# Two turns of a software pipeline written into each pass of the loop, on one Trainium2 core

## The reference

```python
x = layer_norm(inputs); q, k, v = x @ wq, x @ wk, x @ wv          # 16 heads of 16
out_i = phi(q_i) . cumsum(phi(k_j) v_j^T) / (phi(q_i) . cumsum phi(k_j))   # causal, phi = relu + 0.001
x = out @ wo + inputs; x = x + gelu(layer_norm(x) @ w1) @ w2
x = layer_norm(x + ffn(quantise_to_fp6_grid(x)))                   # blocks of 32
q, k, v = silu(conv4(x @ Wq)), silu(conv4(x @ Wk)), silu(conv4(x @ Wv))
delta = chunkwise delta rule over chunks of 32 (inverse of I + A per chunk), 4 heads of 64
short, long = causal FIR filters of 5 and 64 taps on v
y = gated mix of (short, long, delta, v) by an MLP on statistics; y = layer_norm(rms(y) @ Wo + x)
first 1024 tokens: y = layer_norm(y + mixture-of-experts MLP with 2048 hidden)
```

## Time and profile before

| | |
|---|---|
| median of 3 runs | 6195.41 us (6194.68 to 6212.29) |
| profiled execution: its own time | 6197.09 us |
| its span in the profile | 6195.3 us |
| busy: PE, weight loads, DVE, ACT, POOL | 5461.0, 4375.8, 4265.9, 2703.4, 2545.4 us |
| mean granted TensorE clock | 0.915 |

### The profile page before, as it was taken

The page is one execution under the profiler, slowest core; times in us unless marked ns, Lnnn a source line. Parts: engine busy times, 40 slices in busy tenths (PEclk is TensorE's granted clock), DMA queues, the critical chain, the costliest instruction groups (busy, mean ns, idle before and its releaser), DMA issues. The chain is left out here.

```text
span 6195.3 us, 137128 instructions
## 1 busy us (share of the span) xinstructions
PE 5461.0 (88%) x42776; PEld 4375.8 (71%) x42776; DVE 4265.9 (69%) x13841; ACT 2703.4 (44%) x6230; POOL 2545.4 (41%) x3716
## 2 busy tenths in 40 slices
PE   6999999999999999969875528999999999999947
PEld 5888888888888888859844426776767667676734
DVE  4777777777777777732157775887878778787830
ACT  2555555555555555521143313444444444444421
POOL 1222222222222222200087734666666666666640
PEclk9999999999999999979955557999999999999978
DMA  1101110111011101138755522222222222222201
GB/s 40 34 30 34 35 35 28 34 35 35 30 32 35 35 31 32 33 79 193 183 139 134 141 80 66 59 60 60 60 60 60 61 60 60 60 60 60 60 16 41
DMA packets 604094, 374.75 MB, mean 60 GB/s; under 512 B 336528, under 2 KB 589264, under 8 KB 603344
## 3 DMA queue, kind: packets, MB, share of 16 engines
q1 hardware_dynamic: 532880, 329.91, 19.6%
q10 hardware_dynamic: 65664, 16.78, 1.2%
q0 software_dynamic: 4800, 18.88, 1.0%
HBM read 212.59 MB, written 137.10 MB: 56 GB/s over the span
## 5 line engine op out<-in xcount | busy, mean ns | idle before, releaser
L510 POOL TENSOR_TENSOR a_shift<-a_mean_var,a_eps 128x2 f32<-128x2 f32 x256 | 71.3, 279 | 1933.9 <-DVE a_mean_var L725 1933.9
L2141 PE MATMUL c_bank<-c_xT,c_gate 128*128 128x512 f32 x1024 | 508.9, 621 | 17.9 <-issue 16.6
L739 DVE SCALAR_TENSOR_TENSOR a_cv<-a_raw,a_taps,a_cv 128x256 f32<-128x256 f32 x1152 | 461.8, 478 | 20.9 <-DVE a_scaled L668 11.1
L811 PE MATMUL a_bank<-a_w,a_hidden 128*128 128x256 f32 x2048 | 459.2, 383 | 0.9 <-ACT a_hidden L599 0.9
L909 PE MATMUL a_bank<-a_turned,a_w 128*128 128x256 f32 x2048 | 454.4, 380 | 1.3 <-ACT a_turned L558 1.1
L811 PEld LDWEIGHTS a_bank<-a_w,a_hidden 128*128 128x128 f32 x2048 | 384.4, 190 | 71.3 <-issue 20.5
L909 PEld LDWEIGHTS a_bank<-a_turned,a_w 128*128 128x128 f32 x2048 | 384.6, 190 | 54.2 <-ACT a_turned L558 5.1
L1783 POOL TENSOR_TENSOR c_expd<-c_e,c_logit 128x16 f32<-128x16 f32 x128 | 371.7, 2904 | 64.0 <-DVE c_logit L1969 52.8
L1769 POOL TENSOR_TENSOR c_stats<-c_l2sq,half 128x16 f32<-128x16 f32 x128 | 373.5, 2918 | 17.4 <-DVE c_l2sq L1958 17.4
L2145 PEld LDWEIGHTS c_bank<-c_statsT,c_gate_stats 128*128 128x128 f32 x2048 | 271.9, 193 | 126.9 <-issue 126.9
L1343 POOL TENSOR_TENSOR i_coef<-i_base,i_exponent 128x12 f32<-128x12 f32 x128 | 297.8, 2327 | 91.7 <-ACT i_base L1373 87.4
(11 more groups left out here) (295 smaller groups left out, 14072.2 us busy)
## 6 DMA issues: line engine op xcount, KB each, us to landing
a_x<-in_x SPq DMA_DIRECT2D x64, 256.0 KB, 4.0
scratch_xb<-a_xb SPq DMA_DIRECT2D x64, 256.0 KB, 2.1
scratch_q<-a_qkv_rows SPq DMA_DIRECT2D x64, 256.0 KB, 2.2
scratch_k<-a_qkv_rows SPq DMA_DIRECT2D x64, 256.0 KB, 2.5
scratch_v<-a_qkv_rows SPq DMA_DIRECT2D x64, 256.0 KB, 2.8
b_window<-scratch_v SPq DMA_DIRECT2D x8, 2048.0 KB, 22.3
scratch_long<-b_out ACTq DMA_DIRECT2D x8, 2048.0 KB, 24.6
scratch_short<-b_out POOLq DMA_DIRECT2D x8, 2048.0 KB, 18.4
```

The costliest lines, as they stand in the source:

```text
L739: ins = dve.scalar_tensor_tensor(cv[s][:, n, c], raw[s][:, n, c, j:j + TOK], taps[:, n, c, j:j + 1], cv[s][:, n, c], ALU.mult, ALU.add)
L811: ins = pe.matmul(dst[:, t * D:(t + 1) * D], src[s][:, c, tile_cols(t)], weight[:, c], start=(c == 0), stop=(c == chunks - 1))
L2141: pe.matmul(dst[:].rearrange("p (h t) -> p h t", h=H), gate1[:, c, cols], xT[sl][:, c:c + 1].broadcast_to([P, H, P]), start=(c == 0), stop ...
```

## The change

`run_pipelined` writes `written=2` turns into the body of each loop. The loop counts passes from 0, and `(iterations - last) // 2` of them are run: 7 in phase A, 3 in phase I, 3 in phase C. A turn that is left over (one in phase A, one in phase C) is written out behind the loop with constants. `skip` is gone, and `PsumPlan.left_out` takes the jobs that a first or last turn lacks out of the counts.

```diff
+def run_pipelined(eng, order, iterations, stages, link=None, links=None, written=1):
...
-            elif skip is not None:
-                skip(j - late, s, stage)
...
-    with eng.Fori(last, iterations) as j:
+    passes = (iterations - last) // written
+    if passes > 1:
+        with eng.Fori(0, passes) as n:
+            for m in range(written):
+                turn(n * written + (last + m), range(last + 1), base + (n * written + m) * each)
+    for j in range(last + passes * written if passes > 1 else last, iterations):
         turn(j, range(last + 1), base + (j - last) * each)
...
+    def left_out(self, b, turn, rank):
+
+        first = self.turns if not isinstance(turn, int) else turn
+        n = sum(late > t for t in range(min(first, self.turns)) for late in self.lates[b])
+        if not isinstance(turn, int):
+            return n
+        n += sum(late < t - self.iterations + 1 for t in range(self.iterations, turn) for late in self.lates[b])
+        return n + sum(late > turn or late < turn - self.iterations + 1 for late in self.lates[b][:rank])
+
     def free(self, i, s, job):
-        b = self.bank_of[s, job]
-        return (i + self.late[s, job]) * self.uses[b] + (self.base[b] + self.rank[s, job])
+        b, turn, rank = self.bank_of[s, job], i + self.late[s, job], self.rank[s, job]
+        return turn * self.uses[b] + (self.base[b] + rank - self.left_out(b, turn, rank))
...
-        return [base + (iterations + self.turns) * uses for base, uses in zip(self.base, self.uses)]
+        return [base + iterations * uses for base, uses in zip(self.base, self.uses)]
...
-            def skip(i, s, stage):
-
-                for job in jobs_of.get(stage, ()):
-                    b = plan.bank(s, job)
-                    open_bank(i, s, job)
-                    pe.sem_inc(bank_full[b], 1)
-                    pe.sem_inc(bank_read[b], 1)
-
-            run_pipelined(pe, order, batches, stages, skip=skip)
+            run(pe, order, batches, stages)
```

More of the change, by code:

```diff
@@ L11 @@
 from contextlib import ExitStack
+from functools import partial
 import math
@@ L98, in __init__ @@
         self.bank_of, self.rank, self.late, self.uses = {}, {}, {}, [0] * BANKS
+        self.lates = [[] for _ in range(BANKS)]
         for n, (stage, s, late, job) in enumerate(jobs):
@@ L251, in phase_a @@
     T = 2
+    WRITTEN = 2
     DEPTH = 4.779
@@ L271, in phase_a @@
               ("lnB_stats", 1.69), ("lnB", 1.72), ("xbT", 3.97), ("qkv1", 3.91), ("conv", 1.64), ("qkvT", 0.01)]
+    run = partial(run_pipelined, written=WRITTEN)
     order = pipelined(shares, STEPS, DEPTH)
@@ L497, in store_qkv @@
                     sp.dma_start(out_v[name][i * STEPS + s], qkv_rows[s][:, n]).then_inc(qkv_stored[s % OUTS], 16)
-            run_pipelined(sp, order, batches, {"load": load, "lnB": store_xb, "qkvT": store_qkv})
+            run(sp, order, batches, {"load": load, "lnB": store_xb, "qkvT": store_qkv})
             for m in range(OUTS):
@@ L537, in _ @@
             link = Chain(pool, S["pool_chain"])
-            run_pipelined(pool, order, batches, stages, link, links)
+            run(pool, order, batches, stages, link, links)
         @block.scalar
@@ L636, in _ @@
             }
-            run_pipelined(act, order, batches, stages)
+            run(act, order, batches, stages)
         @block.vector
@@ L764, in _ @@
             link = Chain(dve, S["dve_chain"])
-            run_pipelined(dve, order, batches, stages, link, links)
+            run(dve, order, batches, stages, link, links)
         @block.tensor
@@ L1186, in phase_i @@
               ("kT", 0.01), ("gram", 2.87), ("keep", 269.02), ("gather", 11.45), ("inverse", 6.78)]
+    run = partial(run_pipelined, written=WRITTEN)
     order = pipelined(shares, STEPS, DEPTH)
     jobs_of = {"xT": ["xT"], "beta": ["beta"], "kT": ["kT"], "gram": ["G0", "G1"]}
-    plan = PsumPlan(order, jobs_of, banks.count)
+    plan = PsumPlan(order, jobs_of, banks.count, ITERATIONS)
     steps_of = [[0]] + [[2 * s - 1, 2 * s] for s in range(1, STEPS)]
@@ L1327, in store_inverse @@
                       .then_inc(S["inverse_stored"], 16)
-            run_pipelined(sp, order, ITERATIONS, {"load": load, "scale": store_coef, "keep": store_below,
+            run(sp, order, ITERATIONS, {"load": load, "scale": store_coef, "keep": store_below,
                                                   "gather": gather, "inverse": store_inverse})
@@ L1429, in _ @@
             link = Chain(dve, S["dve_chain"])
-            run_pipelined(dve, order, ITERATIONS, {"squares": sums, "keep": keep, "inverse": invert}, link, links)
+            run(dve, order, ITERATIONS, {"squares": sums, "keep": keep, "inverse": invert}, link, links)
         @block.tensor
@@ L1479, in gram @@
                                 fill(ins, s, f"G{o}")
[L1481 to L1489, removed]
+            run(pe, order, ITERATIONS, {"xT": turn_x, "beta": beta, "kT": turn_k, "gram": gram})
     banks.count = plan.after(ITERATIONS)
@@ L1747, in store @@
                     sp.dma_start(xc_v[i], xc[sl][:]).then_inc(xc_stored, 16)
-            run_pipelined(sp, order, TILES, {"load": load, "load_src": load_sources, "lnD": store})
+            run(sp, order, TILES, {"load": load, "load_src": load_sources, "lnD": store})
             for m in range(OUTS):
@@ L1810, in _ @@
             link = Chain(pool, N["pool_chain"])
-            run_pipelined(pool, order, TILES, stages, link, {"rms": 1, "lnC_stats": 3, "lnD_stats": 3})
+            run(pool, order, TILES, stages, link, {"rms": 1, "lnC_stats": 3, "lnD_stats": 3})
         @block.scalar
@@ L1893, in _ @@
                 stages[f"solve{b}"] = solved(b)
-            run_pipelined(act, order, TILES, stages)
+            run(act, order, TILES, stages)
         @block.vector
@@ L2179, in _ @@
                 stages[f"carry{b}"] = carry(b)
[L2181 to L2189, removed]
+            run(pe, order, TILES, stages)
     banks.count = plan.after(TILES)
```

18 lines of the change are left out of this document (10 added, 8 removed).

## The result

The changed kernel takes 6090.74 us (median of 4 runs, 6087.91 to 6109.03) against 6195.05 us (median of 4, 6194.49 to 6212.29): ratio 0.9831, 95% interval 0.9806 to 0.9857. 104 us are gained, 1.7%, where 62 were forecast, and the fast end of the range was 6115 us: the prediction was wrong. Run again later (run 9), the same code gave 0.9852 (0.9834 to 0.9869). The profiled execution took 6089.46 us; its span is 107.6 us shorter than that of the kernel before.

The account below looks back on a forecast made before the run. TensorE was taken to bound phases A and C, with VectorE the engine to watch in phase I. 40.5 + 15.8 + 2 + 0 + 2.3 + 1.5 = 62.1 us off 6195.4 gave 6133 us, range 6115 to 6166 us.

Parts of the forecast that it names:

- In phase C's last turns gaps of up to 0.75 us end at `skip`: End of phase C: dropping `skip` there gains 0 to 2.3 us, taken as 1.5 us.
- The upper bound of `skip`: Start of phase A and phase C's last turns: `skip` gains at most 4.6 us, used for the range's fast end.
- Constants for registers in the turns left over: Turns left over: a few register instructions fewer; with the table load at the head of phase A's body, nothing gained.
- Branches of phase A: Phase A, 14 branches to 6: idle time and low clock, 5.06 us each, 40.5 us, all on TensorE, the path.
- Branches of phase C: Phase C, 6 branches to 2: idle time and low clock, 3.96 us each, 15.8 us gained.
- Phase I, 2 us: Phase I, 5 branches to 2: VectorE's stops give nothing, SyncE's held loads 0 to 4.2 us, taken as 2 us.
- the doubled bodies, 0: TensorE in phase I and perhaps ScalarE in phase A begin to stop at branches; 25 us uncovered, taken as 0.
- the 7.4 us of TensorE's two stops: Phase I: TensorE's doubled body leaves instruction memory, 2 branches of 3.7 us; if uncovered, 7.4 us less gain.
- The start of phase A, 2.3 us: Start of phase A: without `skip`, TensorE reaches line 802 earlier, 2.3 us on the path.
- Half of it: Rival: another engine sets the pace once TensorE does not stop; 45 us gained, 6150 us, chance 0.16.
- Slower: Rival: TensorE's doubled body in phase I is supplied too slowly; 181 us added, about 6315 us, chance 0.02.
- no change: Rival: stops let lagging engines catch up, or TensorE stops inside bodies too; 0 to 15 us, about 6187 us, chance 0.05.

Follow-up runs that it names:

- run 9: The changed kernel run again, unaltered, on the chip of the other experiments: 6103.40 us, ratio 0.9852 to the kernel before.
- run 1: The changed kernel with one turn a pass (`WRITTEN = 1`) in all three phases, `skip` still gone: 6174.63 us, ratio 0.9952 to the kernel before.
- run 7: The changed kernel with 820 more semaphore increments by TensorE, without waits, behind its last turn of phase C: 6218.58 us, ratio 1.0025 to the kernel before.
- run 3: The changed kernel with ScalarE's wait for the stored rows on its own instruction ahead of the table load in `silu_rows`: 6078.37 us, ratio 0.9792.
- run 4: The changed kernel with one turn a pass, and ScalarE's wait for the stored rows on its own instruction ahead of the table load: 6142.00 us, ratio 0.9906.
- Run 10: The changed kernel with ScalarE's wait ahead of the table load and only TensorE's turns all written out: 6067.09 us, ratio 0.9789.
- run 8: The changed kernel with ScalarE's wait ahead of the table load and one taken branch in each of the three phases: 6039.89 us, ratio 0.9742.
- run 5: The changed kernel with ScalarE's wait ahead of the table load and all turns written out on all engines: 6002.36 us, ratio 0.9678.

## Why the prediction was wrong

**The step that failed: "In phase C's last turns gaps of up to 0.75 us end at `skip`; three steps there, 0 to 2.3 us, I take 1.5."** It measured 62 us (the gap in the two profiles) to 63.5 us (run 1), and run 7 gives the same rate without `skip`. I asked where the array waits for `skip`, and the array waits for nothing once its matmuls are done; the price is at the end of the block, which the other engines can't leave before TensorE's sequencer has. I had the price of a pair and for phase I I even worked out what the pairs cost if their cover were gone, 43 us. For phase C I counted no pairs: 206 x 0.305 = 63 us, and nothing else runs beside them. The upper bound of `skip`, 4.6 us for both of its places, shut the true value out; that is why the range failed.

**"Constants for registers in the turns left over: a few register instructions fewer ... Nothing for both."** This failed too, in the other direction, and not by what the instructions cost. I looked at the turns left over alone; the new counts changed the register instructions inside the loop as well. They decided on which instruction a wait stands, and with it when a 1.28 us table load runs. It took back (1958.2 - 1943.0) = 15 us in the twelve turns of phase A (11 us with run 9, where they take 1953.8 us), and 26 us in the whole phase by runs 3 and 9 (2708.7 - 2683.1). I named the table load at the head of the body, and not the other eight of a turn. The same sentence is doubtful for phase I: about 20 us lie between loops and written-out turns there.

The two errors partly cancel in the total, and that is luck: without the late loads (run 3) the change gains 127 us, twice the forecast.

**Branches of phase A, 8 x 5.06 us: right** in mechanism and near in price. There are 6 waits on issue of 3.57 us, run 3 gives 5.0 us a branch, and phase A is 45.8 us shorter in run 3 than in run 4, which differ in the turns a pass alone: 5.7 us for each of the 8 branches. "All of it lies on TensorE, which is the path" is right only while all engines lose their stops together. Run 10 shows that the stops of the others, 2.3 to 2.7 us at VectorE and 2.0 to 2.4 us at ScalarE, keep most of the cost; which of them is not told apart. Taking away TensorE's stop alone would have been forecast at 30 us by my reasoning and gave 7.

**Branches of phase C, 15.8 us: right within what can be told.** One turn a pass gave 2273.3, 2282.2 and 2283.5 us, two turns with the loops on all engines 2246.8, 2251.4, 2257.0, 2267.6 and 2268.9 us. The means, 2279.7 and 2258.3 us, differ by 21 us for 4 branches, 5.3 us each against 3.96 forecast, with a spread of 22 us in the second group. That -26.7 us in the first comparison looked like 6.7 us a branch is partly chance. With everything written out phase C takes 2228.0 and 2236.1 us, 22 to 30 us under the mean for two branches, and one branch (run 8) gives 2255.1 us. That is more than the price of two branches, and what else it is stays open.

**Phase I, 2 us, and the doubled bodies, 0: the total right (-2.2 us; the means of all runs, 621.0 for one turn and 622.3 us for two, say nothing at all).** VectorE's store is what it waits for, as forecast. The stop comes at two boundaries only, and where it doesn't, the wait for the stored inverse is longer: 7.5 to 7.8 us instead of 5.3 to 5.6. In the changed kernel, 3250 to 3604 us, as the earlier trace rows:

```profile
DVE i_T L1419 <- DMA scratch_inverse<-i_T: 34.0, 5, 7.8
...
DVE i_below L1405 <- issue: 6.3, 2, 3.2
```

TensorE's branch in phase I has lost its quickness, as forecast; compare:

```profile
L83 PEldq COMPARE_BRANCH  x3: 83/3418/3429, 3314.7 to 3598.3; - x3
```

The Trainium skill (page "Runtime: NRT & Kernel Launch", section "Instruction fetch mechanics") gives 2048 instructions for TensorE's memory and 512 for the others'. For TensorE the trace agrees: with 1381 recorded instructions between two branches a branch takes 0.22 us, with 2766 it takes 3.4 us. For the other engines the trace differs from 512: in the kernel before, bodies of 313 (SyncE) and 379 (VectorE) in phase I and of 408 (GpSimd) and 465 (ScalarE) in phase C have stops of 2.4 to 5.3 us, while bodies of 83 to 289 instructions in either kernel (SyncE, ScalarE, GpSimd) have none. Whether the 7.4 us of TensorE's two stops were paid can't be told inside the spread of phase I, 617 to 626 us.

The other doubt about the doubled bodies came true as well: ScalarE's body in phase A grows from 222 to 456 instructions, and in the changed kernel it stands 6 times on issue, 15.1 us in all, where it had no such wait before. The cover held as I assumed, since a branch still costs 5.0 us in all (run 3).

**The start of phase A, 2.3 us: right.** In the changed kernel the first `wq` comes 1.11 us behind the matmuls ahead of it and not 3.34 us. Over the whole phase, run 4 is 1.4 us shorter than the kernel before.

**The rivals.** "Half of it" came true in phase A alone, which gave 17.7 of 42.8 us, and for a reason that it didn't name: a table load on ScalarE, not a slow engine. In run 5 GpSimd does hold TensorE in phase C, 25.5 us. "Slower" and "no change" had nothing for them: inside the three loops of the changed kernel TensorE waits on issue only behind taken branches, 6 times in phase A and twice each in phases I and C.

What stays open: where the 20 us come from that phase I gains only when nothing loops, why phase C gains 22 to 30 us then, and what makes the clock lower in phase C in one run than in another.

## What to carry to other kernels

Count the instructions that a sequencer has to get through behind the last useful work of a phase, and multiply by their price, here 0.15 us for a semaphore instruction of TensorE; every engine waits at the end of a block like this one. An idle array in the page's busy tenths at a boundary of phases is the first thing to ask about, before any loop. When an edit changes counts or constants, look at which instruction each wait now stands on, above all next to activation table loads; a wait that is long met, placed ahead of the load, cost one line and gave 25 to 33 us here, and 54 us with all turns written out.

## What the runs showed of the hardware

A semaphore increment of TensorE without a wait is recorded with 51 ns and comes every 0.154 us (820 in 125.9 us). With all turns written out, code that never repeats was supplied in phase A without one wait of the array on issue (run 5, 300 to 2440 us), so its length alone cost nothing there. An engine's stop behind a taken branch reaches the others: with TensorE's loop alone written out, phase A gained 7 of 33 us. Executions of the same code of phase C lie up to 22 us apart, most of it busy time of TensorE's matmuls: more than the whole forecast for its branches.
